# Sharing the pass over the weights' absolute values between ScalarE and VectorE

## The reference

```python
def _weight_quant(w):
    scale = 1.0 / jnp.maximum(jnp.mean(jnp.abs(w)), EPS)
    q = jnp.clip(jnp.round(w * scale), -1.0, 1.0) / scale
    return w + jax.lax.stop_gradient(q - w)

gv = _bitlinear(h, w_gv)      # w_gv: 16384 x 2048, float32
value, gate = jnp.split(gv, 2, axis=-1)
u = value * jax.nn.silu(gate)
out = _bitlinear(u, w_out)    # w_out: 2048 x 8192, float32
```

## Time and profile before

| | us |
|---|---|
| median of 3 runs | 7830.78 |
| lowest and highest of the runs | 7808.51, 7857.8 |
| profiled execution | 7858.54 |
| span of its slowest core (core 0) | 7857.0 |
| spans of its 8 cores | 7777.8 to 7857.0 |

### The profile page before, as it was taken

One profiled execution on the slowest core, in us unless ns is written; L12 is line 12 of the kernel. 1 busy time (PEld: TensorE's weight loads), 2 busy tenths in 40 slices (PEclk: granted clock), 3 DMA queues, 4 the chain that ended last, 5 costly groups with the idle time before them and its releaser, 6 DMA issues.

```text
span 7857.0 us, 49222 instructions; the slowest of 8 cores (7777.8 to 7857.0 us)
## 1 busy us (share of the span) xinstructions
PE 3292.5 (42%) x12882; PEld 1340.3 (17%) x13138; DVE 3952.0 (50%) x3177; ACT 3284.0 (42%) x3227; POOL 180.3 (2%) x343
## 2 busy tenths in 40 slices
PE   2100021110219888988888500000523615346196
PEld 0000000000004333333333200000211202112032
DVE  3600037557474444444444433577776576677612
ACT  2554431212223333333333455466665466456501
POOL 2000000000000000000000000000000000000000
PEclk7555555555559999999999755555766757667577
DMA  7776610010112222222222366211424315233232
GB/s 158 267 268 200 186 52 21 22 42 1 40 38 97 94 94 97 92 96 97 93 95 97 115 198 197 73 62 61 146 78 154 122 66 179 86 113 133 92 124 101
DMA packets 217462, 853.71 MB, mean 109 GB/s; under 512 B 34656, under 2 KB 34656, under 8 KB 159840
## 3 DMA queue, kind: packets, MB, share of 16 engines
q1 hardware_dynamic: 120240, 604.05, 23.4%
q10 hardware_dynamic: 64512, 167.80, 5.7%
q0 software_dynamic: 32432, 78.70, 4.0%
HBM read 694.24 MB, written 167.77 MB: 110 GB/s over the span
## 4 chain that ended last, share of the span: by engine, by line
DVE 44%; ACT 20%; DMA 17%; PE 7%; issue 7%; POOL 2%; ACTq 1%; DVEq 1%; SPq 0%; POOLq 0%
DVE zt L80 16%; DMA ub<-u_sp 5%; DMA wmean<-wgvt 5%; ACT wqt L80 4%; ACT wqs L80 4%; DMA wmean<-woutT 3%; PE pout L1315 3%; DVE res L80 3%; DVE paby L80 3%; DVE Mx L80 3%; ACT wabs L80 3%; DVE sg_t L80 2%; DVE u_r L80 2%; DVE gc_t L80 2%; DMA wo_r<-woutT 2%
## 5 line engine op out<-in xcount | busy, mean ns | idle before, releaser
L1315 PE MATMUL pout<-q_r,qo_r 128*128 128x512 bf16 x4012 | 999.0, 414 | 1094.1 <-ACT mq L80 554.3
L1017 PE MATMUL pvg<-q,qwv 128*128 128x512 bf16 x4014 | 1024.5, 410 | 387.6 <-DVE u_r L80 220.4
L80 DVE SCALAR_TENSOR_TENSOR zt<-mq,zt 128x1024 f32<-128x1024 f32 x896 | 1097.9, 1225 | 160.8 <-DVE zt L80 157.7
L80 ACT ACTIVATE mq<-zt,pbh 128x1024 f32<-128x1024 f32 x896 | 1028.8, 1148 | 229.3 <-DVE zt L80 224.8
L1022 PE MATMUL pvg<-q,qwg 128*128 128x512 bf16 x4014 | 919.9, 379 | 4.3
L80 ACT ACT_TABLE_LOAD x82 | 105.2, 1283 | 1554.4 <-DVE q L80 404.3
L1315 PEld LDWEIGHTS pout<-q_r,qo_r 128*128 128x128 bf16 x4096 | 425.6, 104 | 1671.7 <-issue 1446.3
L1017 PEld LDWEIGHTS pvg<-q,qwv 128*128 128x128 bf16 x4096 | 422.2, 104 | 960.5 <-issue 553.0
L80 ACT ACTIVATE wabs<-wmean 128x2048 f32<-128x2048 f32 (+1 forms) x256 | 379.6, 1483 | 463.2 <-DMA wmean<-wgvt 247.7
L1022 PEld LDWEIGHTS pvg<-q,qwg 128*128 128x128 bf16 x4096 | 400.8, 98 | 483.3
L80 ACT ACTIVATE sg_t<-gc_t 128x512 f32<-128x512 f32 x256 | 161.2, 630 | 553.1 <-DVE gc_t L80 553.1
(11 more groups left out here) (144 smaller groups left out, 3594.6 us busy)
## 6 DMA issues: line engine op xcount, KB each, us to landing
wmean<-wgvt SPq DMA_DIRECT2D x128, 1024.0 KB, 5.6
wld<-wgvt SPq DMA_DIRECT2D x128, 1024.0 KB, 4.9
qo_r<-qo_sp SPq DMA_DIRECT2D x128, 1024.0 KB, 5.9
wmean<-woutT SPq DMA_DIRECT2D x128, 512.0 KB, 4.3
u_sp<-u_r ACTq DMA_DIRECT2D x64, 1024.0 KB, 4.0
wo_r<-woutT SPq DMA_DIRECT2D x128, 512.0 KB, 3.8
ub<-u_sp POOLq DMA_DIRECT2D x256, 256.0 KB, 5.4
qo_sp<-qo_t ACTq DMA_DIRECT2D x128, 256.0 KB, 2.9
```

Source lines behind the costliest of these rows:

```text
L80: r = f(*a, **kw)
L1017: t.matmul(pvg[:, 2 * q * TS:(2 * q + 1) * TS], qwv[:, r * 2048 + k * 128:r * 2048 + (k + 1) * 128], q1[:, (ts * DC + k) * TS:(ts * DC + k ...
L1315: last = t.matmul(pout[:, d * TS:(d + 1) * TS], qo_r[:, base + d * 128:base + (d + 1) * 128], rhs, start=(j == 0), stop=(j == HC - 1))
```

## The change

The tiles with even numbers stay on ScalarE; those with odd numbers are reduced by VectorE, with one `tensor_reduce` that takes absolute values and adds. VectorE's new block stands behind the block of the scan in the code. SyncE's wait before the load of tile i is now for ScalarE's semaphore or for VectorE's, by the parity of i. ScalarE always writes its absolute values to the first half of `wabs`; VectorE writes only the sums. The explicit wait of ScalarE for its own earlier ACTIVATE is gone.

```diff
     abase_w0 = sA.n
+    vbase_w0 = sV.n
 
     @SCA
     def _(sc):
         for i, (_src, width) in enumerate(w0_tiles):
-            sc.wait_ge(rW0.sems[i % 2].h, 16 * (i // 2 + 1))
-            if i >= 2:
-                sc.wait_ge(sA.h, abase_w0 + i - 1)
-            sc.activation(out=wabs[:, (i % 2) * 2048:(i % 2) * 2048 + width],
-                                 in_=wmean[:, (i % 2) * 2048:(i % 2) * 2048 + width],
-                                 func=AF.Abs, accum_out=accW[:, i:i + 1])
+            if i % 2:
+                continue
+            sc.wait_ge(rW0.sems[0].h, 16 * (i // 2 + 1))
+            sc.activation(out=wabs[:, 0:width],
+                          in_=wmean[:, 0:width],
+                          func=AF.Abs, accum_out=accW[:, i:i + 1])
     tok_w0acc = sA.n
+
+    @VEC
+    def _(v):
+        for i, (_src, width) in enumerate(w0_tiles):
+            if i % 2 == 0:
+                continue
+            v.wait_ge(rW0.sems[1].h, 16 * (i // 2 + 1))
+            v.tensor_reduce(out=accW[:, i:i + 1],
+                            in_=wmean[:, 2048:2048 + width],
+                            axis=AX.X, op=ALU.add, apply_absolute_value=True)
+    tok_w0accv = sV.n
 
     @blk.sync
     def _(s):
         s.wait_ge(sMM.h, tok_zg)
         for i, (src, width) in enumerate(w0_tiles):
             if i >= 2:
-                s.wait_ge(sA.h, abase_w0 + (i - 1))
+                if i % 2 == 0:
+                    s.wait_ge(sA.h, abase_w0 + (i - 2) // 2 + 1)
+                else:
+                    s.wait_ge(sV.h, vbase_w0 + (i - 2) // 2 + 1)
             rW0.inc(i, s.dma_start(out=wmean[:, (i % 2) * 2048:(i % 2) * 2048 + width],
                                    in_=src))
```

## The result

| | before | changed |
|---|---|---|
| median, us | 7829.99 (10 runs) | 8070.01 (9 runs) |
| lowest and highest, us | 7808.51, 7857.8 | 8038.89, 8162.19 |
| span of the profiled execution's slowest core, us | 7857.0 (core 0) | 8069.0 (core 3) |
| mean span of the 8 cores, us | 7816.6 | 8046.6 |

The ratio of changed to before is 1.030, with a 95% interval of 1.0281 to 1.0319. The 8162.19 us is one run in a slower state of the chip (granted clock 0.64 on four cores, 0.68 on the others), which the ratio leaves out; without it the highest is 8078.37 us and the median 8067.2 us.

The account below looks back on a forecast made before the run. The weight-mean pass was held bound by its two-slot loop, landing plus read, not by ScalarE. Stall 216, longer slot period +11 and quieter traffic -4 summed to +223 us on the median 7830.8: 8054 us, range 7985 to 8120, 82 in 100.

Parts of the forecast that it names:

- The order on VectorE: VectorE's block runs behind the scan, so tile 3's load waits for tile 1's reduction, which starts at 340.7 us.
- The price of the stall: Load of tile 3 goes out at 343.1 us instead of 126.97, a shift of 216.1 us.
- The reduction: VectorE's wide reduction runs at the one-element rate: 2.29 us for 2048 floats and 1.22 us for 1024.
- Rival D: VectorE's reduction is slow, at the scan's 4.42 us: 220 us in place of 11, 8263 us; 3 in 100.
- The period of a slot: VectorE's slot takes 0.28 us longer per large tile, 0.07 per small: 0 to 22 us, taken as +11.
- quieter traffic: The 55 tiles formerly read beside the scan now run at 3.93 instead of 4.00 us each: -4 us.
- a worse landing time: One ground, with a partial C, for extending the forecast range up to 8120 us; no size of its own.
- rival C: The two slots' loads go out and land together: 195 us on top, 8249 us, DMA share below 0.65; 3 in 100.
- The meant gain: Two engines reading relieve ScalarE, but the tiles did not wait for ScalarE; costed at nothing.
- Rival A: Two readers let slots reach least landing time: +126 us, 7957 us; second estimate, from GpSimd's DMA fit, near 7895; 8 in 100.
- Rival B: The load stream saturates the DMA engines at 341 GB/s behind the stall: pass ends 65 us sooner, 7766 us; 2 in 100.
- Rival E: No stall, as reductions run in between the scan's operations: 7842 us, no change; 2 in 100.

Follow-up runs that it names:

- the stall alone: Kernel before with one added wait: the load of tile 3 waits for the scan's last operation, all tiles on ScalarE; 8044 us, 1.0265 of before.
- the reads in turn: Changed kernel with ScalarE's and VectorE's reads each made to wait for the other's read of the tile before; 8040 us, 1.0262 of before.
- a spaced start: Changed kernel with one more wait: the load of tile 4 waits until tile 3 has landed; 8047 us, 1.0279 of before.
- the split without the stall: Changed kernel's split put late: tiles 0 to 55 all on ScalarE, odd tiles from 56 on on VectorE; 7822 us, 0.9981 of before.
- the four slots: Kernel before with four slots in the ring instead of two, all tiles on ScalarE; 7572 us, 0.9673 of before.
- The late bunch: Odd tiles on VectorE only from 56 on, plus tile 60's load waiting until tile 59 is read; 7828 us, 0.9997 of before.
- the second measurement of the changed kernel: Changed kernel run once more, unaltered, for a second profile; 8060 us, 1.0270 of the kernel before.

## Why the prediction was right, and where it was off

Forecast were 8054 us and slower by 223 us; it came to 8070 us, slower by 240 us by the medians.

*The order on VectorE.* Right, as the timeline above and the stall alone show. The first wide reduction started at 340.7 us in the mean of the cores, as forecast for core 0 (at 342.30 us on core 3), and SyncE's wait was 218.0 us (forecast some 212: it begins when tile 2 has gone out, at 126.23 us). On core 3 ScalarE read on at 353.4 us, not at 348: tile 4's load goes out right behind tile 3's and lands after it.

*The price of the stall.* 216 us forecast, 216 us between the mean times of tile 3's load. The stall alone cost 208 us with its faster tiles behind it, where forecast were 210. The skip of the scan's cover was not made good later: behind the pass the stages were as long as before.

*The reduction.* 2.29 and 1.22 us were forecast from the slope of the two-input operations and the 285 ns of the small reduction; 2.286 and 1.220 us were measured. Rival D is out.

*The period of a slot.* This is the term that was mis-sized. I gave +11 us, out of 0 to 22, for VectorE's longer read, and -4 us for quieter traffic, +7 us in all. Measured were +28 us for the large tiles and -5 us for the small ones, +23 us. That is above what these terms allowed, -4 to 18 us. The time lay well inside the range all the same, because the stall is nine tenths of the loss and because I had widened the range for "a worse landing time" without giving it a size; on that side it was luck. The longer read alone was not it, since with the reads in turn or with a spaced start VectorE reads as long, and most of the 28 us were gone. What took longer was the landing. I had asked whether ScalarE's queue held the tiles back, and it did not; I had put the landing time down as unchanged. In the changed kernel (core 3) the reads come in pairs:

```profile
611.91 2.29 DVE L80 TENSOR_REDUCE accW<-wmean 128x1 f32<-128x2048 f32 x1 [6.38 <-DMA wmean<-wgvt]
...
615.74 1.91 ACT L80 ACTIVATE wabs<-wmean 128x2048 f32<-128x2048 f32 x1 [7.39 <-DMA wmean<-wgvt]
...
620.08 2.29 DVE L80 TENSOR_REDUCE accW<-wmean 128x1 f32<-128x2048 f32 x1 [5.88 <-DMA wmean<-wgvt]
622.69 1.91 ACT L80 ACTIVATE wabs<-wmean 128x2048 f32<-128x2048 f32 x1 [4.94 <-DMA wmean<-wgvt]
...
629.04 2.29 DVE L80 TENSOR_REDUCE accW<-wmean 128x1 f32<-128x2048 f32 x1 [6.68 <-DMA wmean<-wgvt]
631.50 1.91 ACT L80 ACTIVATE wabs<-wmean 128x2048 f32<-128x2048 f32 x1 [6.81 <-DMA wmean<-wgvt]
```

The two reads of a pair are 3.8, 2.6 and 2.5 us apart, with 4.3 and 6.4 us until the next pair. In the stall-alone kernel (core 5) the reads are 3.9 and 3.8 us apart at the same place:

```profile
603.72 1.91 ACT L80 ACTIVATE wabs<-wmean 128x2048 f32<-128x2048 f32 x1 [1.53 <-DMA wmean<-wgvt]
...
607.62 1.91 ACT L80 ACTIVATE wabs<-wmean 128x2048 f32<-128x2048 f32 x1 [1.90 <-DMA wmean<-wgvt]
...
611.45 1.91 ACT L80 ACTIVATE wabs<-wmean 128x2048 f32<-128x2048 f32 x1 [1.83 <-DMA wmean<-wgvt]
```

The pairing is rival C in a mild form: landing rose to 6.2 us and the DMA share fell to 0.68, short of the 0.65 that I had named as its sign, and it cost 28 and not 195 us. My ground against C, that the loads queue and come apart by themselves, fits pairs whose reads stay 2.3 us or more apart, and was wrong in that they go no further on most cores. Why they don't is open. One engine that reads everything can't start two large reads less than 2.1 us apart, but that is no explanation: in the changed kernel none came closer than 2.31 us, and the kernel before has such pairs itself.

*The meant gain.* Costed at nothing, and nothing was found for the large tiles: no two of their reads overlapped, and with the split but no stall the last 70 took 283 us, where they had taken 276. For the small tiles there were 5 to 7 us in the mean of the cores against the kernel before, and 2 to 4 us against the stall alone; of their 127 pairs of neighbouring reads at most three overlapped on any core, in the changed kernel and in the split without the stall.

*Rival A* did not come: landing got longer, not shorter. (Its second estimate leaves out the 0.14 us that the first one has until the read starts; with them the time would be near 7910 us and not 7895.) *Rival B* came, but by another way: the DMA engines were filled by two more slots. The limit that I had named, landing plus read in each of two slots, is what the four slots took away. The full rate was 339 GB/s at a share of 1.00, against 341 worked out beforehand. The Trainium skill, in "DMA: Bandwidth & Descriptors", section "Specifications", has some 358 GB/s of HBM per core; the measured 339 is 5% below that. *Rival E* needed another order in the code; with the split put late, its time of 7842 us was even undercut by 20 us.

**What stays open.** What decides whether a pair of cores runs in the slow pace is not settled. Counted were 14 cores of 16 in it for the changed kernel, 2 of 8 each for reads in turn, for a spaced start, for the split without the stall and for the kernel before, and none for the stall alone. Most cores were in it only where a second reader and a start with two loads at once came together; by what means is not shown. The late bunch had both too, with ScalarE's tile first, and left all cores out. That the pace is shared by neighbouring cores points to something that they share; this was only argued from the pairs, and no run held one core of a pair apart. By the total time alone the changed kernel and the stall-alone kernel are barely told apart (1.030 and 1.027 in two measurements against 1.0265), and neither are the reads in turn or the spaced start told from the second measurement of the changed kernel; the 25 to 28 us rest on the traces of single executions.

## What to carry to other kernels

Work given to an idle engine starts where it stands in that engine's order, not when its data is there: look at what is in front of it while the other engines count on it, here 218 us of scan in front of a 2.3 us reduction that every further load waited for. Before sharing reads between engines, see what ended the reader's idle time; where it was the transfer in 254 of 256 cases, the lever is more transfers in flight, and two more slots gave 3.3% where the second reader, placed behind the scan, cost 3.0%. To see whether a second reader can help at all, look for reads that overlap: here, for the large tiles, there were none. And don't take a landing time as fixed when the loads start in another rhythm; here it went from 5.5 to 6.2 us, for a reason that stayed open.

## What the runs showed of the hardware

Landing time and rate went opposite ways. With four loads of 1 MiB in flight landing took 10.2 us in the median and the rate was 339 GB/s at a DMA share of 1.00; with two it took 5.5 us and the rate was 266 GB/s at 0.78 (core 0 of the kernel before, behind the scan). And the two-slot loop had two paces, 5.4 to 5.7 and 5.9 to 6.3 us of landing for the same tiles, which neighbouring cores always shared and could leave in the middle of a pass. I had expected one value with a spread.
